# Counting edges into an adjacency matrix with other one-hots: source modulo 128 stationary, 640 keys moving

## The chip, the cores and the metric

The kernel runs on one core of one Trainium2 chip. The metric is device time in microseconds (us) for one execution, compared by the median of several runs.

## The reference, cut to what matters

Four graph layers are applied in turn, each joined to its input and normalized. All of them add up rows over the same 21250 edges, sorted by destination. The third layer tells two relations apart by `edge_type_2`.

```python
out = jax.ops.segment_sum(norm[:, None] * xw[row], col, num_segments=n)      # layer 0
agg = jax.ops.segment_sum(h[src], dst, num_segments=1250)                    # layer 1
deg = jax.ops.segment_sum(jnp.ones_like(dst), dst, num_segments=1250)
msg = jnp.where((edge_type == 0)[:, None], msgs[0], msgs[1])                 # layer 2, edge_index = (src, dst)
agg = jax.ops.segment_sum(msg, row, num_segments=1250)
x   = h + jax.ops.segment_sum(h[send], rec, num_segments=1250)               # layer 3
```

The features are 512 wide, the nodes 1250 (10 tiles of 128, padded to 1280). The weights of two relations are mixed from 30 bases: `w = einsum('rb,bio->rio', att, basis)`.

## The kernel before, in words

The kernel does not gather rows. It first builds the matrix of edge counts and then does every aggregation as a dense matmul with it. Two forms are needed: `A[p, r, t, n]`, counts for relation r with node `t*128 + p` on the partitions, and `AT`, the transposed counts summed over the relations with the identity added on the diagonal.

The counting stage works through windows of destinations. An edge list of 170 chunks of 128 edges lies in SBUF, one edge of each chunk on each partition. `window_range` (L381) reads a table that VectorE has computed: the first chunk of a window, how many pairs of chunks it spans, and a running number of pairs. For each pair VectorE writes one-hots into one of `OH` = 4 slots (`windows`, L1041): `oh_dst`, 128 wide, one-hot of destination within the window of 64 and relation; `oh_src`, 1280 wide, one-hot of the source. TensorE multiplies them (`pair_product`, L506): `oh_dst` is stationary, `oh_src` moves, and the product adds up in PSUM, 128 rows of (relation, destination) by 1280 sources, in two sets of three banks. A semaphore `s_ohu` gives slots back to VectorE, `s_oh` gives them to TensorE. ScalarE copies the finished window into `A` (`window_out`, L702) and takes the degrees `dg` as a by-product. After two windows a tile of 128 destinations is complete; TensorE turns it block by block by a matmul with the identity (`turn_counts`, L527) and ScalarE copies the result into `AT` (`turned_out`, L709).

Between the windows TensorE mixes the first layer's bases: 120 float32 products (`mix`, L543), 15 of them ahead of the first window, five after each window and the rest behind the last. They read bases that SyncE's queue brings into eight slots. VectorE also has reductions over x and W0 between windows (L1145 to L1163), ScalarE splits x into two halves, and GpSimd forms the low halves (L484, L467). Behind the stage come the unit 0 dense tiles (`dense`, L589), of which the first waits for the last mixing product's eviction, a table load and the turned input. Each engine executes its instructions in the order written; a loop over windows or pairs is a real loop with register arithmetic and a branch, and the addresses of slots and chunks are computed in registers.

Of the kernel before, what the change touches and what calls it, by code (L numbers as in the profile page):

```python
# [6 lines left out]
N, D, E = 1250, 512, 21250  # L7
# [6 lines left out]
WIN = 64  # L14
# [12 lines left out]
MIX_WIN = 5  # L27
# [16 lines left out]
def resnorm_gnn_kernel(nc, x, src_t, dst_t, typ_t, dst_r, W0, b0, gamma, beta,  # L44
# [11 lines left out]
    with ctx:  # L56
# [27 lines left out]
        dg = sb("dg", [P, REL, NT], f32)  # L84
# [28 lines left out]
        epsc = sb("epsc", [P, 1], f32)  # L113
        b0T = sb("b0T", [P, KT], f32)
# [20 lines left out]
        oh_src = zview(2 * NP * 2 * OH)  # L135
        oh_dst = zview(2 * P * 2 * OH)
        iota_n = hview(2 * NP)
        code = hview(2 * P)
        negw = hview(4 * NWIN).bitcast(f32)
        src_i, dst_i, typ_i = (wview(4 * CHUNKS).bitcast(i32) for _ in range(3))  # L140
        src_f, key_f = (wview(4 * CHUNKS).bitcast(f32) for _ in range(2))
        HC = CHUNKS // 2
        dstr = hview(4 * 2 * P).bitcast(i32).rearrange("p (g e) -> p g e", g=2)
        wlo = wview(4 * NWIN).bitcast(f32)
        whi = wview(4 * NWIN).bitcast(f32)
        cid = wview(4 * 4).bitcast(f32)
        mnx = wview(4 * 4).bitcast(f32)
        fl = wview(4 * 2 * NWIN).bitcast(f32)
# [7 lines left out]
        zview(4 * NWIN)  # L156
        mix_in = [zview(4 * D).bitcast(f32) for _ in range(MIX_SLOTS)]
# [52 lines left out]
        s_gin = sem("s_gin")  # L210
        s_xc = sem("s_xc")
# [58 lines left out]
        def tile_moved(eng, s, t, j):  # L270

            if not isinstance(t, int) or t >= 0:
                eng.wait_ge(s[j], (t + (2 - j)) * 8)

# [100 lines left out]
        Z_SCALED = 37  # L375
# [62 lines left out]
        def _(pool):  # L438
# [6 lines left out]
            pool.iota(negw, [[-2 * WIN, NWIN]], base=0, channel_multiplier=0, **kw).then_inc(s_const, 1)  # L445
            pool.iota(code, [[1, REL], [2, WIN]], base=0, channel_multiplier=0, **kw).then_inc(s_const, 1)
            pool.iota(iota_n, [[1, NP]], base=0, channel_multiplier=0, **kw).then_inc(s_const, 1)
# [6 lines left out]
            pool.memset(epsc[:, :], EPS).then_inc(s_const, 1)  # L454
            pool.memset(ones, 1.0).then_inc(b_one, 1)
# [48 lines left out]
        def _(pe):  # L504

            def pair_product(ready, slot, j, start, stop):  # L506

                pe.wait_ge(s_oh, ready)
                for q in range(2):
                    for c in range(0, NP, D):  # L510
                        w = min(D, NP - c)
                        last = nc.tensor.matmul(Df[:, j, c:c + w], oh_dst[:, ds(slot * (2 * P) + q * P, P)],  # L512
                                                oh_src[:, ds(slot * (2 * NP) + (q * NP + c), w)],
                                                start=start and q == 0, stop=stop and q == 1)
                last.then_inc(s_win if stop else s_ohu, 1)

            def window(w, j):
                _, pairs, base = window_range(pe, w)
                wait(pe, s_wev, w * 2 - 2)
# [7 lines left out]
            def turn_counts(t, g, bank=T[:, 0, :]):  # L527

                pe.wait_ge(s_wev, t * 4 + 4)
                wait(pe, s_ate, t * 3 + g)  # L530
                for q, m in enumerate(range(4 * g, min(4 * g + 4, NT))):
                    if m == t:
                        nc.tensor.matmul(bank[:, q * P:(q + 1) * P], ident[:, :], ident[:, :], start=True, stop=False)
                    for r in range(REL):
                        last = nc.tensor.matmul(bank[:, q * P:(q + 1) * P],  # L535
                                                A[:, r, ds(t, 1), m * P:(m + 1) * P].rearrange("p a c -> p (a c)"),
                                                ident[:, :], start=(r == 0 and m != t), stop=(r == REL - 1))
                last.then_inc(s_at, 1)

# [16 lines left out]
            pe.wait_ge(s_const, 9)  # L556
            pe.wait_ge(s_tbl, 1)
            for t in range(NT):
                window(2 * t, 0)
                if t:  # L560
                    turn_counts(t - 1, 0)
                mix(MIX_WIN - 2)
                if t:
                    turn_counts(t - 1, 1)
# [855 lines left out]
```

## Time and profile before

| | us |
|---|---|
| median of 3 runs (1015.02 to 1017.96) | 1015.09 |
| the profiled execution | 1016.28 |
| its span | 1014.5 |
| TensorE busy | 967.5 |
| VectorE busy | 669.1 |
| ScalarE busy | 365.7 |

The span runs from the first to the last instruction of the profiled execution; the execution's own time lies 1.8 us above it. "Busy" counts the instructions of an engine that do work, not its register, branch and semaphore instructions.

### The profile page before, as it was taken

What the parts mean: (1) busy time and instruction counts of PE and PEld (TensorE: products, weight loads), DVE (VectorE), ACT (ScalarE), POOL (GpSimd) and SP (SyncE); (2) the same over time, 40 slices, a digit from 0 to 9 for tenths busy, and PEclk for the clock granted to TensorE, in tenths of its full rate; (3) what the DMA queues carried; (4) which work ended last, traced back from release to release, by engine and by line L of the source; (5) the groups of instructions that cost most, each with busy time, mean ns of one, the idle gap of its engine ahead of it and who ended that gap; (6) DMA issues with size and microseconds to landing.
All of it is one profiled execution on the core that took longest, in us unless ns stands there. A gap on an engine that the chain in (4) does not pass through costs nothing.

```text
span 1014.5 us, 15078 instructions
## 1 busy us (share of the span) xinstructions
PE 967.5 (95%) x4904; PEld 472.2 (47%) x4904; DVE 669.1 (66%) x1262; ACT 365.7 (36%) x520; POOL 85.2 (8%) x66
## 2 busy tenths in 40 slices
PE   6899999998999799998999899999999999999997
PEld 2444444444555554444444344444444444445443
DVE  5776767664243767999999999999233334542258
ACT  0224344545587442344313322111632231144342
POOL 1000011111011100210211100000400010010000
PEclk9999999999999899999999999999999999999999
DMA  8634443444211115565553155551001003110014
GB/s 276 231 116 132 131 123 114 145 135 126 95 42 43 52 55 195 163 217 191 169 174 102 64 158 146 175 145 53 1 21 42 1 22 114 63 42 1 1 52 154
DMA packets 59445, 108.59 MB, mean 107 GB/s; under 512 B 6497, under 2 KB 6966, under 8 KB 59386
## 3 DMA queue, kind: packets, MB, share of 16 engines
q1 hardware_dynamic: 38522, 68.45, 22.0%
q10 hardware_dynamic: 20864, 39.33, 11.9%
q8 instruction: 40, 0.66, 0.3%
q14 instruction: 19, 0.16, 0.0%
HBM read 95.24 MB, written 12.52 MB: 106 GB/s over the span
## 4 chain that ended last, share of the span: by engine, by line
PE 78%; DVE 14%; DMA 3%; issue 2%; ACT 2%; POOL 1%; DVEq 0%; ACTq 0%; SPq 0%
PE Dp L610 25%; PE Dp L637 23%; PE T L551 11%; PE Dp L512 10%; PE Dp L662 4%; DVE acc L1128 4%; PE T L584 2%; PE T L535 1%; DVE stt L1219 1%; PE Dp L672 1%; DVE Zraw L1238 1%; DVE w L1256 1%; DMA Zraw<-in_basis 1%; DVE mcol L1082 1%; DVE acc L1283 1%
## 5 line engine op out<-in xcount | busy, mean ns | idle before, releaser
L610 PE MATMUL Dp<-W,hT 128*128 128x512 f16 x1320 | 296.9, 381 | 5.9 <-ACT hT L821 4.6
L610 PEld LDWEIGHTS Dp<-W,hT 128*128 128x128 f16 x1320 | 127.0, 98 | 150.9 <-ACT hT L821 6.6
L637 PE MATMUL Dp<-Zraw,A 128*128 128x512 f16 x800 | 173.3, 379 | 0.0
L1128 DVE SCALAR_TENSOR_TENSOR acc<-stage,att,acc 128x512 f32<-128x512 f32 x232 | 168.1, 792 | 1.4 <-DMA stage<-in_basis 1.4
L637 PE MATMUL Dp<-Zraw,AT 128*128 128x512 f16 x600 | 130.8, 379 | 0.5 <-DVE Zraw L1196 0.5
L551 PE MATMUL T<-Zraw,W 128*128 128x512 f32 x240 | 114.6, 615 | 10.8 <-DVE W L1011 8.5
L637 PEld LDWEIGHTS Dp<-Zraw,A 128*128 128x128 f16 x800 | 78.2, 98 | 93.9
L512 PE MATMUL Dp<-Zraw 128*128 x594 | 111.6, 343 | 3.9 <-issue 3.3
L1056 DVE TENSOR_SCALAR Zraw<-hT,w 128x1280 f16 x198 | 102.7, 561 | 0.0
L821 ACT ACTIVATE hT<-T 128x1024 f16<-128x1024 f32 x70 | 71.5, 1021 | 85.0 <-PE T L584 80.1
L1050 DVE SCALAR_TENSOR_TENSOR Zraw<-w,hT 128x256 f16 x99 | 49.8, 503 | 65.4 <-PE Dp L512 46.6
L637 PEld LDWEIGHTS Dp<-Zraw,AT 128*128 128x128 f16 x600 | 58.5, 98 | 71.0 <-DVE Zraw L1196 0.9
L512 PEld LDWEIGHTS Dp<-Zraw 128*128 x594 | 58.0, 98 | 63.0 <-issue 18.1
L1196 DVE SCALAR_TENSOR_TENSOR Zraw<-Dp,zsc,Zraw 128x512 f16<-128x512 f32 x30 | 22.5, 749 | 77.2 <-ACT Zraw L875 77.2
L1256 DVE SCALAR_TENSOR_TENSOR w<-Dp,aggc,S 128x512 f32<-128x512 f32 x40 | 29.8, 745 | 64.6 <-PE Dp L637 58.7
L705 ACT ACTIVATE A<-Dp 64x1280 f16<-64x1280 f32 x40 | 49.2, 1229 | 57.8 <-PE Dp L512 57.3
L551 PEld LDWEIGHTS T<-Zraw,W 128*128 128x128 f32 x240 | 43.5, 195 | 55.3 <-issue 44.8
L875 ACT ACTIVATE Zraw<-Dp,zsc 128x512 f16<-128x512 f32 x50 | 32.2, 686 | 92.3 <-PE Dp L610 92.0
L610 PE MATMUL Dp<-Zraw,hT 128*128 128x512 f16 x240 | 57.1, 394 | 7.1 <-ACT hT L821 6.2
L915 ACT ACTIVATE w<-w,s_in 128x512 f32<-128x512 f32 x30 | 21.6, 722 | 116.1 <-DVE w L1256 116.1
L467 POOL TENSOR_TENSOR W<-wst,W 128x1024 f16<-128x1024 f32 x18 | 42.2, 2364 | 168.2 <-ACT W L771 168.2
L584 PE MATMUL T<-ident,S 128*128 128x128 f16 x560 | 43.1, 220 | 3.9 <-ACT hT L821 3.2
(158 smaller groups left out, 772.2 us busy)
## 6 DMA issues: line engine op xcount, KB each, us to landing
Zraw<-in_basis SPq DMA_DIRECT2D x120, 256.0 KB, 3.0
stage<-in_basis SPq DMA_DIRECT2D x120, 256.0 KB, 2.9
xres<-w ACTq DMA_DIRECT2D x30, 256.0 KB, 2.0
xr<-xres ACTq DMA_DIRECT2D x30, 256.0 KB, 2.6
wst<-in_Wn ACTq DMA_DIRECT2D x4, 1024.0 KB, 5.6
wst<-in_Ws ACTq DMA_DIRECT2D x4, 1024.0 KB, 5.5
wst<-mixd ACTq DMA_DIRECT2D x4, 1024.0 KB, 5.4
wst<-in_root ACTq DMA_DIRECT2D x3, 1024.0 KB, 6.1
```

Of the source, the lines that this page charges most:

```text
L467: pool.tensor_tensor(weights_of(u, m)[:, 1, 2 * h:2 * h + 2, :], source, weights_of(u, m)[:, 0, 2 * h:2 * h + 2, :], ALU.subtract).then_in ...
L512: last = nc.tensor.matmul(Df[:, j, c:c + w], oh_dst[:, ds(slot * (2 * P) + q * P, P)], oh_src[:, ds(slot * (2 * NP) + (q * NP + c), w)], s ...
L551: nc.tensor.matmul(T[:, 1, :], mixT[:, b * P:(b + 1) * P], mix_in[n % MIX_SLOTS], start=(b == 0), stop=(b == PAIRS - 1)).then_inc(s_mx, 1)
L584: last = nc.tensor.matmul(T[:, h, k * P:(k + 1) * P], S16[:, ds(t, 1), h * D + k * P:h * D + (k + 1) * P] .rearrange("p a c -> p (a c)"), ...
L610: last = nc.tensor.matmul(Dp[:, j, m, :], hT[:, j, hp, k * P:(k + 1) * P], weights_of(u, m)[:, wp, k, :], start=(n == 0), stop=(n == 3 * K ...
L637: last = nc.tensor.matmul(sum_bank(t), a[:, k, ds(t * P, P)], Z[:, r, h, k, :], start=(n == 0), stop=(n == count - 1))
L662: last = nc.tensor.matmul(Df[:, j, c:c + w], Z[:, 0, h, k, b * P:(b + 1) * P], AT[:, k, c:c + w], start=(k == 0 and h == 0), stop=(k == NT ...
L705: nc.scalar.activation(A[WIN * j:WIN * (j + 1), r, ds(t, 1), :], Dp[WIN * r:WIN * (r + 1), j, :, :].rearrange("p j d -> p (j d)")[:, 0:NP] ...
L821: nc.scalar.activation(hT[:, j, :, :], T[:, :, :], ACT.Copy).then_inc(s_hT, 1)
L1050: v.scalar_tensor_tensor(oh_dst[:, ds(slot * (2 * P), 2 * P)].rearrange("p (c o) -> p c o", c=2), key_f[:, ds(c, 2)].rearrange("p (c o) -> ...
L1056: last = v.tensor_scalar(oh_src[:, ds(slot * (2 * NP) + q * NP, NP)], iota_n, src_f[:, ds(c + q, 1)], None, ALU.is_equal)
L1128: last = v.scalar_tensor_tensor(part, stage[:, q, :], a, part, ALU.mult, ALU.add)
```

## The change

The one-hots are cut in another way. The stationary one-hot `oh_lo` is 128 wide and marks the source modulo 128. The moving one-hot `oh_key` is 640 wide and marks a key, `20*destination + 2*(source tile) + relation`, within a window of now 32 destinations. A product has 128 rows (source within its tile) and 640 columns in two banks of 320. There are 40 windows instead of 20. A window is therefore already transposed: ScalarE copies it into a buffer `B` (two tiles deep), from which TensorE turns each relation into `A` (five steps of four blocks for a tile), and VectorE adds the two relations of `B` into `AT` and then the identity (`sum_counts`). The degrees come from ten matmuls of `AT` with a column of ones (`degrees`). The mixing products are spread evenly over the windows (`mix_share`), two or three after each.

```diff
-WIN = 64
+WIN = 32
+PER = P // WIN
+KEYS = WIN * REL * NT
+HALF = KEYS // 2
+COUNT_STEPS = ((0,), (1, 2), (3,), (4,))
...
+        def mix_share(w):
+
+            rest = PAIRS * (GROUPS - 1)
+            return (w + 1) * rest // NWIN - w * rest // NWIN
...
 # pair_product, TensorE
                 for q in range(2):
-                    for c in range(0, NP, D):
-                        w = min(D, NP - c)
-                        last = nc.tensor.matmul(Df[:, j, c:c + w], oh_dst[:, ds(slot * (2 * P) + q * P, P)],
-                                                oh_src[:, ds(slot * (2 * NP) + (q * NP + c), w)],
+                    for b in range(2):
+                        last = nc.tensor.matmul(Dp[:, j, b, 0:HALF], oh_lo[:, ds(slot * (2 * P) + q * P, P)],
+                                                oh_key[:, ds(slot * (2 * KEYS) + (q * KEYS + b * HALF), HALF)],
                                                 start=start and q == 0, stop=stop and q == 1)
...
+            def turn_counts(t, g, bank):
+
+                pe.wait_ge(s_wev, PER * (t + 1))
+                for r in range(REL):
+                    for i in range(2):
+                        last = nc.tensor.matmul(bank[:, (2 * r + i) * P:(2 * r + i + 1) * P], B[:, t % 2, 2 * g + i, r, :],
+                                                ident[:, :], start=True, stop=True)
                 last.then_inc(s_at, 1)
+
+            def degrees(t):
+
+                pe.wait_ge(s_sum, 2 * t + 2)
+                for m in range(NT):
+                    last = nc.tensor.matmul(DG[:, 2 * t:2 * t + 2], AT[:, m, t * P:(t + 1) * P], onec[:, :],
+                                            start=(m == 0), stop=(m == NT - 1))
+                last.then_inc(s_deg, 1)
...
+            for w in range(NWIN):
+                window(w, w % 2)
+                t = w // PER - 1
+                if t >= 0:
+                    for g in COUNT_STEPS[w % PER]:
+                        wait(pe, s_ate, 5 * t + g - 1)
+                        turn_counts(t, g, count_bank(t, g))
+                    if w % PER == 2:
+                        degrees(t)
+                mix(mix_share(w))
...
+            def window_out(w):
+
+                t, a = w // PER, (w % PER) * WIN
                 act.wait_ge(s_win, w + 1)
...
+                nc.scalar.activation(B[:, t % 2, :, :, a:a + WIN].rearrange("p s r (b d) -> p b (s r) d", b=2),
+                                     Dp[:, w % 2, 0:2, 0:HALF].rearrange("p b (d k) -> p b k d", k=REL * NT),
+                                     ACT.Copy).then_inc(s_wev, 1)
...
 # windows, VectorE
-                        v.scalar_tensor_tensor(oh_dst[:, ds(slot * (2 * P), 2 * P)].rearrange("p (c o) -> p c o", c=2),
-                                               key_f[:, ds(c, 2)].rearrange("p (c o) -> p c o", o=1).broadcast_to([P, 2, P]),
-                                               negw[:, ds(w, 1)],
-                                               code.rearrange("p (c o) -> p c o", c=1).broadcast_to([P, 2, P]),
-                                               ALU.add, ALU.is_equal)
                         for q in range(2):
-                            last = v.tensor_scalar(oh_src[:, ds(slot * (2 * NP) + q * NP, NP)], iota_n,
-                                                   src_f[:, ds(c + q, 1)], None, ALU.is_equal)
+                            v.tensor_scalar(oh_lo[:, ds(slot * (2 * P) + q * P, P)], iota_n[:, 0:P],
+                                            lo_f[:, ds(c + q, 1)], None, ALU.is_equal)
+                            last = v.tensor_scalar(oh_key[:, ds(slot * (2 * KEYS) + q * KEYS, KEYS)], iota_n,
+                                                   wkey[:, ds(w, 1)], key_f[:, ds(c + q, 1)], ALU.add, ALU.is_equal)
                         last.then_inc(s_oh, 1)
+
+            def sum_counts(t):
+
+                own = AT[:, t, t * P:(t + 1) * P]
+                dve.wait_ge(s_wev, PER * (t + 1))
+                v.tensor_tensor(AT[:, :, t * P:(t + 1) * P], B[:, t % 2, :, 0, :], B[:, t % 2, :, 1, :], ALU.add).then_inc(s_sum, 1)
+                dve.wait_ge(s_sum, 2 * t + 1)
+                v.tensor_tensor(own, own, ident[:, :], ALU.add).then_inc(s_sum, 1)
```

`sum_counts(t)` is called by VectorE before the third window of the tile behind t (windows 6, 10, ..., 38), and for the last tile behind all windows. Windows 6 to 9 and 13 are written out singly, the others stand in loops over two to four windows. The last tile's turns stand behind dense tiles 0 and 2 of unit 0, `degrees(9)` behind tile 0, and the square root of the degrees in ScalarE's first dense step.

The next rows are VectorE's instruction stream for one pair inside the loop over windows, from the head of the loop over pairs to its branch. This is the kernel before; "ISA", "REGISTER_ALU" and the branch are register and control rows, and "x2" stands for two alike.

```order
L1044 ISA
L1050 REGISTER_ALU
L1050 ISA
L1050 REGISTER_ALU
L1050 ISA x2
L1050 SCALAR_TENSOR_TENSOR Zraw<-w,hT 128x256
L1056 ISA
L1056 TENSOR_SCALAR Zraw<-hT,w 128x1280
L1056 ISA
L1056 TENSOR_SCALAR Zraw<-hT,w 128x1280
L1044 ISA
```

Behind these follow one register row and one branch (14 in all). The same place in the changed kernel:

```order
L1085 ISA
L1092 REGISTER_ALU
L1092 ISA
L1092 REGISTER_ALU
L1092 ISA
L1092 TENSOR_SCALAR Zraw<-hT,w 128x128
L1094 ISA x2
L1094 TENSOR_SCALAR Zraw<-hT,w 128x640
L1092 ISA
L1092 TENSOR_SCALAR Zraw<-hT,w 128x128
L1094 ISA
L1094 TENSOR_SCALAR Zraw<-hT,w 128x640
```

Behind these stand one control row, one register row and the branch (16 in all). One operation and one address row have come in for each pair; a window that is written out singly has one address row less in either kernel (13 before, 15 now).

The other place is VectorE between two windows at the end of the reductions over x. Before, between windows 6 and 7 (a row's waits stand in brackets):

```order
L1155 TENSOR_REDUCE xcol<-xr 128x1
L1158 TENSOR_REDUCE xin<-xcol 128x1 [waits s_xc]
L1042 UNCONDITIONAL_BRANCH
L383 TENSOR_LOAD tbl
L383 ISA x2
```

And in the changed kernel, between windows 9 and 10:

```order
L1213 TENSOR_REDUCE xcol<-xr 128x1
L1216 TENSOR_REDUCE xin<-xcol 128x1 [waits s_xc]
L1102 TENSOR_TENSOR AT<-Zraw 128x10x128 [waits s_wev]
L1104 TENSOR_TENSOR AT<-AT,ident 128x128 [waits s_sum]
L1083 UNCONDITIONAL_BRANCH
L1083 ISA
L406 TENSOR_LOAD tbl
L406 ISA x2
```

The two additions of `sum_counts(1)` stand ahead of the next windows' table read and one-hots; at the seven later places (before windows 14, 18, ..., 38) they stand the same way, with no reduction in front.

## Rows read from the trace of the kernel before

**Rows 1.** The page, part 1: span, and busy time and share of TensorE.

```profile
span 1014.5 us, 15078 instructions
...
PE 967.5 (95%) x4904; PEld 472.2 (47%) x4904; DVE 669.1 (66%) x1262; ACT 365.7 (36%) x520; POOL 85.2 (8%) x66
```

**Rows 2.** Stretches: length, busy us (instructions) of each engine, clock, DMA share, GB/s.

```profile
24.00:43.50 19.50, 16.50 (x72) 7.46 (x69) 12.73 (x31) 3.25 (x5) 0.00 (x0) 1.00 0.76 262
...
160.00:241.00 81.00, 78.46 (x375) 39.14 (x373) 52.97 (x103) 40.26 (x61) 13.13 (x9) 1.00 0.41 123
```

**Rows 3.** Groups by line, 0 to 290 us: busy us, mean ns, idle before.

```profile
L551 PE MATMUL T<-Zraw,W 128*128 128x512 f32 x240 | 114.6, 615 | 10.8 <-DVE W L1011 8.5 <-PE Dp L512 0.9 <-DMA Zraw<-in_basis 0.4
L512 PE MATMUL Dp<-Zraw 128*128 x594 | 111.6, 343 | 3.9 <-issue 3.3 <-DVE Zraw L1056 0.6
L1056 DVE TENSOR_SCALAR Zraw<-hT,w 128x1280 f16 x198 | 102.7, 561 | 0.0
...
L1050 DVE SCALAR_TENSOR_TENSOR Zraw<-w,hT 128x256 f16 x99 | 49.8, 503 | 65.4 <-PE Dp L512 46.6 <-issue 12.3 <-PEq L525 1.8
```

**Rows 4.** The chain of waits, 164 to 205 us: start, us, what.

```profile
170.37 5.42 PE Dp L512 x30
175.80 0.14 issue
175.93 2.81 PE T L551 x6
...
178.97 1.77 PE T L551 x4
...
186.45 0.61 PE T L535 x8
```

**Rows 5.** VectorE in order of time, 172 to 177 us: start, us, line, operation, [idle before].

```profile
172.06 0.49 DVE L1050 SCALAR_TENSOR_TENSOR Zraw<-w,hT 128x256 f16 x1 [2.95 <-PE Dp L512]
...
174.62 0.48 DVE L1050 SCALAR_TENSOR_TENSOR Zraw<-w,hT 128x256 f16 x1 [1.14 <-PE Dp L512]
175.02 1.01 DVE L1056 TENSOR_SCALAR Zraw<-hT,w 128x1280 f16 x2
176.16 0.48 DVE L1050 SCALAR_TENSOR_TENSOR Zraw<-w,hT 128x256 f16 x1
```

**Rows 6.** VectorE in order of time, first window: first pair, third and fourth.

```profile
18.72 0.48 DVE L1050 SCALAR_TENSOR_TENSOR Zraw<-w,hT 128x256 f16 x1 [2.08 <-issue]
...
22.62 0.48 DVE L1050 SCALAR_TENSOR_TENSOR Zraw<-w,hT 128x256 f16 x1 [0.33 <-issue]
...
24.38 0.48 DVE L1050 SCALAR_TENSOR_TENSOR Zraw<-w,hT 128x256 f16 x1 [0.34 <-issue]
```

**Rows 7.** VectorE in order of time, two pairs of a singly written window.

```profile
55.15 0.48 DVE L1050 SCALAR_TENSOR_TENSOR Zraw<-w,hT 128x256 f16 x1
...
56.58 0.48 DVE L1050 SCALAR_TENSOR_TENSOR Zraw<-w,hT 128x256 f16 x1
```

**Rows 8.** VectorE in order of time around the maximum of W0.

```profile
37.67 0.48 DVE L1050 SCALAR_TENSOR_TENSOR Zraw<-w,hT 128x256 f16 x1 [1.94 <-PE Dp L512]
...
41.73 0.15 DVE L1072 TENSOR_REDUCE mw<-mcol 128x1 f32<-128x1 f32 x1
43.28 0.49 DVE L1050 SCALAR_TENSOR_TENSOR Zraw<-w,hT 128x256 f16 x1 [1.39 <-issue]
```

**Rows 9.** All engines in order of time, end of the counting stage.

```profile
230.25 2.88 DVE L1056 TENSOR_SCALAR Zraw<-hT,w 128x1280 f16 x2
...
235.32 1.00 DVE L1056 TENSOR_SCALAR Zraw<-hT,w 128x1280 f16 x2
...
241.55 6.23 PE L551 MATMUL T<-Zraw,W 128*128 128x512 f32 x14
...
252.58 4.44 PE L610 MATMUL Dp<-W,hT 128*128 128x512 f16 x12
```

**Rows 10.** Groups by line, VectorE, whole span: an addition-like operation of two inputs.

```profile
L1301 DVE TENSOR_TENSOR Zraw<-Dp,W 128x1280 f32<-128x1280 f32 x4 | 6.0, 1492 | 21.2 <-PE Dp L662 21.2
```

More of the change, by code:

```diff
@@ L113, in resnorm_gnn_kernel @@
         epsc = sb("epsc", [P, 1], f32)
+        onec = sb("onec", [P, 2], f16)
         b0T = sb("b0T", [P, KT], f32)
@@ L154, in resnorm_gnn_kernel @@
         w_c = [zview(4 * NWIN).bitcast(f32) for _ in range(2)]
-        zview(4 * NWIN)
-        mix_in = [zview(4 * D).bitcast(f32) for _ in range(MIX_SLOTS)]
+        mix_in = [zview(4 * D).bitcast(f32) for _ in range(3)]
+        zview(2 * (2 * NT * D) - (2 * KEYS * 2 * OH + 2 * P * 2 * OH + 5 * 4 * NWIN + 3 * 4 * D))
+        B = zview(2 * 2 * NT * REL * P).rearrange("p (j s r c) -> p j s r c", j=2, s=NT, r=REL)
+        mix_in += [zview(4 * D).bitcast(f32) for _ in range(MIX_SLOTS - 3)]
         W2 = W[:, 2, :, :, :].rearrange("p h k d -> p (h k d)")
@@ L374, in resnorm_gnn_kernel @@
         XS_FROM = 4
-        Z_SCALED = 37
+        Z_SCALED = 40
         def halves_split(u):
@@ L618, in dense @@
                             back(BACK[t, m])
-                    if u == 0 and t < 3:
-                        turn_counts(NT - 1, t, Dp[:, 1, 2, :])
-                    if u == 0 and t == 3:
+                    if u == 0 and t == 0:
+                        degrees(NT - 1)
+                        for g in range(3):
+                            turn_counts(NT - 1, g, LAST_BANKS[g])
+                    if u == 0 and t == 2:
+                        for g in range(3, 5):
+                            pe.wait_ge(s_ate, 5 * (NT - 1) + g - 2)
+                            turn_counts(NT - 1, g, LAST_BANKS[g - 3])
+                    if u == 0 and t == 5:
+                        pe.wait_ge(s_ate, 5 * NT)
                         spread()
@@ L893, in first_z @@
                     z_out(t, j)
-                    if u == 0 and t < 3:
-                        turned_out(NT - 1, t, Dp[:, 1, 2, :])
-                    if u == 0 and t == 4:
+                    if u == 0 and t in (0, 2):
+                        for g in range(3) if t == 0 else range(3, 5):
+                            turned_out(NT - 1, g, LAST_BANKS[g % 3])
+                    if u == 0 and t == 6:
                         act.wait_ge(b_row, 1)
@@ L1141, in weight_work @@
                         scales(*what)
-            windows(0, 2)
+            windows_to(4)
             for u in (1, 3, 5):
@@ L1148, in _ @@
             weight_work("counts", 0, 0)
-            windows(2, 3)
+            windows_to(6)
             dve.wait_ge(e_x, 48)
@@ L1158, in _ @@
             v.tensor_reduce(xin[:, :], xcol[:, :], AX.X, ALU.max).then_inc(s_xin, 1)
-            windows(7, 8)
+            windows_to(13)
             dve.wait_ge(s_xmax, 1)
```

145 lines of the change are left out of this document (71 added, 74 removed).

## The prediction

> **What bounds the kernel now.** The page says it first: TensorE is busy 95% of a span of 1014.5 us, VectorE 66% [rows 1]. That is an average, so I read the stretches next. Between 160 and 241 us, in the middle of the counting stage that the change rewrites, TensorE works 78.46 of 81 us and VectorE 52.97; ScalarE works 40.26 [rows 2]. The groups of this stage show what fills TensorE: the matmuls of the one-hot pairs (L512, six to a pair, 99 pairs) and the float32 mixing of the bases (L551) [rows 3]. In the chain of waits one window of five pairs takes 5.42 us, so 1.08 us a pair, then a change-over of 0.14 us, then mixing, whose products come as two passes of 0.443 us, so 0.885 us each; the turns cost 0.61 us for eight, 0.076 us each [rows 4]. No wait for VectorE stands in that chain. The stage is TensorE's.
>
> VectorE, however, is not fast, only hidden. I read its order of time, and this is what decides the case. Within a window its pairs start 1.54 us apart (174.62, 176.16), and the first pair of the next window starts 2.56 us after the last pair of the one before (172.06, 174.62), which makes the change of window worth 1.02 us [rows 5]. The pair at 174.62 is listed as waiting for TensorE, but TensorE began this window at 170.37 and was through with the second pair, whose slot this one takes, by 172.5 [rows 4]; the cause is VectorE's own register, table and branch rows. At the start of the stage, where nothing is held back, pairs start 1.76 us apart and the engine stands idle 0.33 us in each ("issue") [rows 6]. In windows that are written out singly the distance is 1.43 us [rows 7]. So the pitch is not the length of the arithmetic. The first operation is over for its follower after 0.40 us (174.62, 175.02), two long ones of 1280 columns take 1.01 us together [rows 5], 0.56 us for one alone [rows 3], so starts 0.45 us apart; 0.40 + 0.45 + 0.45 = 1.30 us would do. What sets the pitch is the engine's own instruction stream.
>
> **The change part by part.** *Matmuls of the pairs.* A pair streams 2 x 2 x 320 = 1280 columns instead of 2560, so 0.54 us by [rows 4]. The reference's index arrays, sorted by destination, give three pairs to every one of the 40 windows: 120 in place of 99. TensorE's pairs go from 99 x 1.08 = 107 us to 120 x 0.54 = 65 us. Turns: 20 a tile where there were 21 with the diagonal, equal. New degree products, 90 inside the stage at 0.076 us or less: +7. Twenty more change-overs at 0.14 us: +3. TensorE alone would therefore save 42 - 10 = 32 us.
>
> *VectorE's pair.* Three operations become four: 128, 640, 128, 640 columns. Their arithmetic is shorter. The stream is longer: in the loop over windows 16 rows in place of 14, with one more address row and one more operation (the order shown above, row for row). One row is priced twice: 1.54 us over 14 rows is 0.11 us, and the step from the singly written loop of 13 rows to the one of 14 is 1.54 - 1.43 = 0.11 us [rows 5, 7]. Two rows more give 1.54 + 0.22 = 1.76 us a pair. Bounds: if the pushed operation costs nothing, 1.65 us; if all windows run as the first do, 1.76 + 0.22 = 1.98 us [rows 6]. I take 1.76 us for the 99 pairs in loops over several windows, 1.65 us for the 15 in windows written out singly, 1.98 us for the first six: 174.2 + 24.8 + 11.9 = 210.9 us.
>
> The opposite reading would be that register rows run behind the arithmetic of the queue, and the idle 0.33 us and the steady 1.54 us speak against it. The Trainium skill, "Advanced Engine Details and Errata", section Sequencer and Instruction Queues, states just that reading: engine instructions can be read and queued while control instructions execute. By it the pitch would be the arithmetic alone, which is the engine-paced rival below; this trace does not agree, with 1.54 us where 1.30 would do.
>
> *VectorE's change of window.* 39 instead of 19, each 1.02 us [rows 5]: 39.8 us.
>
> *The relation sum.* New on VectorE: for each of the ten tiles an addition of 128x1280 in f16, then the diagonal block, which waits for it. What follows a waiting operation shows how expensive such a stop is: after L1072 at 41.73 the next one-hot starts at 43.28, 1.55 us later, because the loop's rows only begin then [rows 8]. A sum costs its own time D, the 0.05 us to the second addition, about 0.5 us to close the old loop and that 1.55 us, less the 1.71 us that a change of window takes anyway from the last long operation's start on (2.56 less 0.40 and 0.45): D + 0.4. D is not in the trace. Nearest above: 1.49 us, the same width in f32 from PSUM [rows 10]; nearest below: 0.5 us, one of the two 1280-wide operations [rows 5]. It is f16 with two inputs, between them; I take 1.0. Nine sums inside the stage: 9 x 1.4 = 12.6 us (8 to 17). The Trainium skill, "VectorE: DVE Perf Modes", the perf-mode tier table, gives 1224 ns for 2048 elements of two 16-bit inputs in SBUF; by an estimate from that page D would be 0.8 us and the nine sums 10.8 us. No run here shows it.
>
> *Stops that were hidden.* The largest absolute value of W0 and its reduction stand between the pairs at 37.67 and 43.28, 5.61 us where 1.43 + 1.02 = 2.45 would do: 3.2 us [rows 8]. The reduction for x and the scales are two more such stops, 2.0 and 2.5 us by the same reckoning. Together 7.7 us; now TensorE's backlog covers them, afterwards nothing does.
>
> *GpSimd.* While it forms the low half of W0, two 1280-wide operations take 2.88 us instead of 1.01 [rows 9]. All four one-hot operations will be of that kind; 2 us for the collisions.
>
> *ScalarE.* 40 evictions of 640 columns instead of 40 of 1280, 50 evictions of the turned counts instead of 30. With 40 of 81 us busy now it stays far from the bound [rows 2]. No term.
>
> *Sum.* VectorE starts at 18.72 [rows 6]; one doubling step more for 40 windows, 0.4. End of its last pair: 19.1 + 210.9 + 39.8 + 12.6 + 7.7 + 2.0, less 0.5 because the last pair needs no loop end = 291.6 us, where it now is 236.3 (235.32 + 1.00) [rows 9]. TensorE follows 0.7 us later, turns (0.3) and has three products of mixing left (2.7): 295.3 us. Today the mixing ends at 241.55 + 6.23 = 247.8 [rows 9], with 14 passes after the last window; the new code spreads them, so part of VectorE's lateness is filled. Difference +47.5 us. The way from there to the first dense tile (252.58 - 247.8 = 4.8 us, [rows 9]) keeps its parts: an eviction, two DMA issues, a table load, an eviction. The degrees now come over TensorE, VectorE and ScalarE behind the first dense tile: +1, since the second tile has another bank and covers the rest. After that nothing changes. 1016.3 (the profiled execution; 1014.5 its span) + 48.5 = 1064.8. The median of the runs shown is 1.2 us lower, so 1063.5.
>
> **The rivals.** *Engine-paced (ends faster).* If VectorE's register rows hide behind its arithmetic, two starts of 640 columns at half of 0.45 to 0.45 us and two of 128 at somewhat less make a pair of 0.9 to 1.4 us, nearer the first. It then stays ahead of TensorE, and the 32 us come home: 1016.3 - 32 - 1.2 = 983. The point where it turns: the 47.5 us above vanish when the 210.9 us of pairs become 163, 1.36 us a pair. For it: the arithmetic is really shorter. Against it: the stage's steady pitch lies 0.24 us above its arithmetic, and idle "issue" stands in the first windows [rows 5, 6].
>
> *Break-even.* A pair at 1.3 to 1.4 us gives no change. It would need four operations and 16 rows to be quicker than three and 13 at 1.43 us [rows 7].
>
> *All windows in the slow pitch.* 114 pairs x 0.22 = +25 us: 1088. For it: rows 6 are rows of this same loop, at a time when VectorE was likewise the late one. Against it: 1.54 us holds in all later windows.
>
> *The clock falls.* With VectorE late, TensorE idles near 29% of the stage. At 1.2 GHz every tile of ten products of mixing and twelve pairs takes nearly twice its 18.9 us (12 x 0.54, 10.5 x 0.885, 30 x 0.076, four change-overs), 37 us against VectorE's 26.6 (12 x 1.76, 4 x 1.02, one sum): +95 us or so, 1160. Against it: between 24 and 43.5 us TensorE is in that situation already (16.50 busy of 19.50) and the granted clock stays 1.00 [rows 2].
>
> **How the numbers follow.** Forecast, VectorE bound by its instruction stream at 1.65 to 1.9 us a pair: 0.68, own range 1048 to 1078. Slow pitch throughout: 0.16. Cheaper rows, 1.45 to 1.65 us, 1022 to 1048: 0.06. Clock: 0.02. Engine-paced or near it: 0.06. Unchanged: 0.02. The range leaves out the clock, the faster case and half of the cheap one: 1040 to 1092. A difference under 0.3%, 3 us, cannot be told from none here. Slower 0.92, same 0.02, faster 0.06.
>
> **What would show it.** In the profile after, the pairs' first operation should start 1.65 to 1.9 us apart with idle "issue" between the operations; from one window's last pair to the next 2.7 to 2.9; the counting stage should end near 295 us, TensorE idle for about 30% of it, released by VectorE; pairs' matmuls at 0.54 us. The chain of waits should name VectorE in the stage where it named TensorE. Wrong would be: a pitch near 1.0 to 1.3 us, TensorE still in the chain, or a stage end below 248.

## The result, and the profile after

The kernel got slower, by about what was forecast. Its median is 1062.57 us (4 runs, 1061.3 to 1062.73) against 1015.15 us for the kernel before on the same chip (4 runs, 1015.02 to 1017.96): a ratio of 1.0456, interval 1.0441 to 1.0471. The prediction said 1063.5 us in a range of 1040 to 1092, with 0.92 for slower. The profiled execution took 1062.55 us.

I read the page of the changed kernel first: span, busy time of each engine, and the shares of the chain that ended last.

```profile
span 1060.7 us, 15792 instructions
...
PE 966.7 (91%) x4880; PEld 471.0 (44%) x4880; DVE 692.2 (65%) x1470; ACT 351.8 (33%) x501; POOL 84.5 (8%) x66
...
PE 63%; DVE 16%; issue 7%; DVEq 7%; DMA 3%; ACT 3%; POOL 0%; ACTq 0%; SPq 0%; PEldq 0%
```

TensorE's busy time looks unchanged (966.7 us, it was 967.5 [rows 1]), although the pairs stream half the columns. That is misleading, and the stretches show why (length, busy us and instructions of TensorE, its weight loads, VectorE, ScalarE and GpSimd, then clock, DMA share, GB/s; the changed kernel):

```profile
124.00:132.00 8.00, 7.73 (x32) 3.84 (x32) 4.88 (x16) 1.30 (x2) 0.00 (x0) 0.59 0.27 78
160.00:240.00 80.00, 65.30 (x306) 32.17 (x304) 52.59 (x156) 25.41 (x41) 7.61 (x7) 0.89 0.39 116
```

In the middle of the counting stage the granted clock is 0.89 where it was 1.00 [rows 2], and for some stretches it is at the lower of its two levels: 0.50 from 123.7 to 130.5 us, which gives the 0.59 of the eight microseconds from 124. Ten such stretches between 31.5 and 263.6 us add up to 58 us. So part of the "busy" time is the same work done slowly. Even with that, TensorE is busy 65.30 us of 80 there, where it was 78.46 of 81.

The groups by line of the changed kernel, 0 to 300 us (busy us, mean ns, then idle before it and what ended it):

```profile
L577 PE MATMUL T<-Zraw,W 128*128 128x512 f32 x240 | 134.1, 698 | 17.4 <-DVE W L1048 8.5 <-DMA Zraw<-in_basis 5.6 <-ACT gw L753 2.7
L534 PE MATMUL Dp<-Zraw 128*128 x480 | 84.5, 315 | 37.3 <-DVE Zraw L1094 33.4 <-issue 3.6
L1092 DVE TENSOR_SCALAR Zraw<-hT,w 128x128 f16 x240 | 65.5, 273 | 92.3 <-issue 66.6 <-PE Dp L534 16.3 <-PEq L547 9.4
```

Three figures carry the reading. The pairs' matmuls (L534) now wait 33.4 us for VectorE's one-hots; before, the pairs' matmuls waited 0.6 us for them [rows 3]. VectorE's low one-hots (L1092) have 92.3 us of idle time ahead of them, of which 66.6 us are "issue": no wait that the profile shows held the engine back; the chain below shows its own register and branch rows there. Mixing, whose code is the same, went from 114.6 [rows 3] to 134.1 us of busy time for the same 240 matmuls; that is the clock: 40 of the 240 fall in stretches at the lower level, where the median of one is 1.06 us instead of 0.59.

Next I put VectorE's instructions of the changed kernel in order of time (start, duration, line, operation, [idle before it and what ended it]). The stretch holds a change of window, a pair, a second pair, a relation sum and what follows it:

```profile
186.33 0.26 DVE L1092 TENSOR_SCALAR Zraw<-hT,w 128x128 f16 x1 [0.47 <-issue]
...
189.06 0.26 DVE L1092 TENSOR_SCALAR Zraw<-hT,w 128x128 f16 x1 [1.49 <-PE Dp L534]
189.34 0.45 DVE L1094 TENSOR_SCALAR Zraw<-hT,w 128x640 f16 x1
189.70 0.25 DVE L1092 TENSOR_SCALAR Zraw<-hT,w 128x128 f16 x1
189.86 0.44 DVE L1094 TENSOR_SCALAR Zraw<-hT,w 128x640 f16 x1
190.78 0.25 DVE L1092 TENSOR_SCALAR Zraw<-hT,w 128x128 f16 x1 [0.48 <-issue]
...
192.50 0.26 DVE L1092 TENSOR_SCALAR Zraw<-hT,w 128x128 f16 x1 [0.47 <-issue]
...
193.65 0.82 DVE L1102 TENSOR_TENSOR AT<-Zraw 128x1280 f16<-128x1280 f16 x1
194.50 0.23 DVE L1104 TENSOR_TENSOR AT<-AT,ident 128x128 f16<-128x128 f16 x1
196.13 0.26 DVE L1092 TENSOR_SCALAR Zraw<-hT,w 128x128 f16 x1 [1.41 <-issue]
```

Each pair has two L1092 rows; the first of them marks the pair's start, and the distance from one pair's start to the next is called the pitch here. Pairs start 1.72 us apart (189.06, 190.78, 192.50), the change of window takes 2.73 us (186.33 to 189.06), and one with a sum in it 3.63 us (192.50 to 196.13). The four operations need only 0.28 + 0.36 + 0.16 + 0.36 us from start to start, the last taken as the second; the rest of each pair, about 0.5 us, is idle.

The profile also shows what stands in that idle time. In the chain of waits (start, us, what; "DVEq" is VectorE's sequencer, with its register, address and branch rows) the pair at 189.06 ends like this:

```profile
189.95 0.13 issue
190.09 0.18 DVEq L1085
...
190.57 0.16 DVEq L1092
```

Between the two long rows stand three short ones of L1092 (0.04, 0.08 and 0.04 us from 190.32, 190.39 and 190.50). The last address row ends at 190.73, and the next pair's one-hot starts at 190.78.

The chain of waits says the same by engine: issue 7% and VectorE's sequencer (DVEq) 7% stand in it now. In the chain of the kernel before, TensorE had 78% and issue 2%, and its counting stage went from one TensorE product to the next [rows 4]. Between 174.7 and 189.1 us the new chain still runs over TensorE, on the strength of the name behind the wait at 189.06; further down stands why that name misleads.

The end of the counting stage, all engines in order of time, in the changed kernel:

```profile
287.37 0.44 DVE L1094 TENSOR_SCALAR Zraw<-hT,w 128x640 f16 x1
288.27 0.73 PE L534 MATMUL Dp<-Zraw 128*128 x4 [1.06 <-DVE Zraw L1094]
...
289.52 2.79 PE L577 MATMUL T<-Zraw,W 128*128 128x512 f32 x6
...
297.11 3.40 PE L633 MATMUL Dp<-W,hT 128*128 128x512 f16 x9
```

VectorE's last pair ends at 287.81 us, the mixing at 289.52 + 2.79 = 292.31, and the first dense tile starts at 297.11. Before, these were 236.3, 247.8 and 252.58 us [rows 9]. So 44.5 of the 46.2 us that the span grew have arisen by the first dense tile, and VectorE was the late engine.

### The profile page after: what moved, and what is told of

The parts are those of the page before. It is cut to its first block, busy times and chain, and to the rows that moved or that the text cites. A ratio compares the mean times of both kernels' runs of the same rounds, so it can differ in the third digit from the quotient of the medians.

```text
span 1060.7 us, 15792 instructions
## 1 busy us (share of the span) xinstructions
PE 966.7 (91%) x4880; PEld 471.0 (44%) x4880; DVE 692.2 (65%) x1470; ACT 351.8 (33%) x501; POOL 84.5 (8%) x66
## 4 chain that ended last, share of the span: by engine, by line
PE 63%; DVE 16%; issue 7%; DVEq 7%; DMA 3%; ACT 3%; POOL 0%; ACTq 0%; SPq 0%; PEldq 0%
PE Dp L633 26%; PE Dp L667 22%; PE T L577 5%; PE Dp L692 4%; DVE acc L1186 3%; DVEq L1092 3%; PE T L607 2%; DVE Zraw L1094 2%; PE Dp L534 2%; DVEq L1085 2%; DVE Zraw L1092 2%; DVEq L1094 1%; DVEq L406 1%; DVE stt L1278 1%; DVE mcol L1140 1%
## 5 line engine op out<-in xcount | busy, mean ns | idle before, releaser
L577 PE MATMUL T<-Zraw,W 128*128 128x512 f32 x240 | 134.1, 698 | 17.4 <-DVE W L1048 8.5
L1092 DVE TENSOR_SCALAR Zraw<-hT,w 128x128 f16 x240 | 65.5, 273 | 92.3 <-issue 66.6
L534 PE MATMUL Dp<-Zraw 128*128 x480 | 84.5, 315 | 37.3 <-DVE Zraw L1094 33.4
L1094 DVE TENSOR_SCALAR Zraw<-hT,w 128x640 f16 x240 | 112.5, 469 | 3.6 <-issue 0.8
L534 PEld LDWEIGHTS Dp<-Zraw 128*128 x480 | 48.3, 101 | 93.3 <-issue 74.8
L740 ACT ACTIVATE Zraw<-Dp 128x640 f16<-128x640 f32 x40 | 28.2, 704 | 180.4 <-PE Dp L534 180.4
L577 PEld LDWEIGHTS T<-Zraw,W 128*128 128x128 f32 x240 | 48.8, 220 | 67.3 <-issue 50.8
L950 ACT ACTIVATE w<-w,s_in 128x512 f32<-128x512 f32 x30 | 21.6, 721 | 116.4 <-DVE w L1315 116.4
```

Source lines behind the costliest of these rows:

```text
L534: last = nc.tensor.matmul(Dp[:, j, b, 0:HALF], oh_lo[:, ds(slot * (2 * P) + q * P, P)], oh_key[:, ds(slot * (2 * KEYS) + (q * KEYS + b * H ...
L577: nc.tensor.matmul(T[:, 1, :], mixT[:, b * P:(b + 1) * P], mix_in[n % MIX_SLOTS], start=(b == 0), stop=(b == PAIRS - 1)).then_inc(s_mx, 1)
L1092: v.tensor_scalar(oh_lo[:, ds(slot * (2 * P) + q * P, P)], iota_n[:, 0:P], lo_f[:, ds(c + q, 1)], None, ALU.is_equal)
L1094: last = v.tensor_scalar(oh_key[:, ds(slot * (2 * KEYS) + q * KEYS, KEYS)], iota_n, wkey[:, ds(w, 1)], key_f[:, ds(c + q, 1)], ALU.add, AL ...
```

## The experiments

All ratios are against the kernel before on the same chip. Theory A is the prediction's: the pairs' pitch is set by VectorE's own instruction stream. Its rivals are arithmetic (the operations' lengths) and waiting for TensorE or for a buffer.

**Arithmetic taken away.** Each key one-hot writes 64 columns instead of 640; the slots are set to zero once at the start. Rows of the stream, waits, matmuls and everything behind them stay. The counts leave out most edges.

```diff
-  last = v.tensor_scalar(oh_key[:, ds(slot * (2 * KEYS) + q * KEYS, KEYS)], iota_n,
+  last = v.tensor_scalar(oh_key[:, ds(slot * (2 * KEYS) + q * KEYS, 64)], iota_n[:, 0:64],
```

> The changed kernel with every key one-hot cut from 640 to 64 columns; the other 576 columns of each slot stay zero, so most edges are not counted. The rows of VectorE's stream stay the same, its arithmetic shrinks. If the instruction stream sets the pitch, pairs stay 1.72 us apart and the time is within 3 us of 1062.6. If the arithmetic sets it, each 640-wide operation falls from 0.36 us to about 0.16 between starts, a pair from 1.72 to 1.3 us, and 120 pairs give back 45 us or more: 1015.

Measured: 1059.28 us (1056.86 to 1060.56), before 1016.38, ratio 1.0419 (1.0397 to 1.044). VectorE in order of time, one pair and the next's start:

```profile
189.56 0.25 DVE L1093 TENSOR_SCALAR Zraw<-hT,w 128x128 f16 x1 [0.77 <-issue]
189.83 0.30 DVE L1095 TENSOR_SCALAR Zraw<-hT,w 128x64 f16 x1
...
191.26 0.25 DVE L1093 TENSOR_SCALAR Zraw<-hT,w 128x128 f16 x1 [0.77 <-issue]
```

The key one-hot's own row fell from 0.45 to 0.30 us, and the idle time grew from 0.48 to 0.77 us: the pairs still start 1.70 to 1.74 us apart. Operations that need nothing like 1.7 us do not start sooner. The stage starts 0.6 us later, because the slots are cleared first, and still the first dense tile comes 2.4 us earlier (294.68 against 297.11). Two single places account for 2.5 of these 3.0 us: a wait for a free slot at 36 us that is shorter by 1.5 us, and the collision with GpSimd at 269 us, shorter by 1.0 us. Arithmetic is ruled out as what sets the pitch.

**Rows taken away.** The two low one-hots of a pair are formed by one operation of 256 columns, as the kernel before forms its source one-hots. Two rows of the stream less in each pair; the result is the same.

```diff
+  v.scalar_tensor_tensor(oh_lo[2 chunks], lo_f[:, ds(c, 2)] broadcast, 0.0,
+                         iota_n[:, 0:P] broadcast, ALU.add, ALU.is_equal)
   for q in range(2):
-      v.tensor_scalar(oh_lo[one chunk], iota_n[:, 0:P], lo_f[:, ds(c + q, 1)], None, ALU.is_equal)
       last = v.tensor_scalar(oh_key[one chunk], iota_n, ...)
```

> The changed kernel with both 128-wide one-hots of a pair written by one operation of 256 columns: 14 rows of the stream for a pair instead of 16, three operations instead of four, but about 0.1 us more arithmetic (0.40 us to its follower instead of two times 0.16). Stream theory: pitch 1.72 - 0.2 = 1.5 us, 120 pairs, 1062.6 - 22 = 1040. Arithmetic theory: 1062.6 + 10 = 1073.

Measured: 1038.77 us (1037.13 to 1040.89), before 1016.38, ratio 1.0216 (1.0199 to 1.0233), 23.8 us less than the changed kernel. VectorE in order of time:

```profile
187.80 0.42 DVE L1091 SCALAR_TENSOR_TENSOR Zraw<-w,hT 128x256 f16 x1 [0.56 <-issue]
188.15 0.80 DVE L1097 TENSOR_SCALAR Zraw<-hT,w 128x640 f16 x2
189.34 0.43 DVE L1091 SCALAR_TENSOR_TENSOR Zraw<-w,hT 128x256 f16 x1 [0.39 <-issue]
...
190.85 0.42 DVE L1091 SCALAR_TENSOR_TENSOR Zraw<-w,hT 128x256 f16 x1 [0.38 <-issue]
```

Pairs start 1.51 to 1.54 us apart. That is the kernel before's pitch of 1.54 us [rows 5] with the same number of rows, though its long operations had 1280 columns and these have 640.

**Rows added.** One more operation of two columns at the head of each pair, into a spare buffer, with its address row; the result is the same.

```diff
+  v.tensor_scalar(spare[:, ds(slot * 2, 2)], iota_n[:, 0:2], lo_f[:, ds(c, 1)], None, ALU.is_equal)
   for q in range(2):
```

> The changed kernel with one more operation a pair, two columns wide, into two spare columns: two more rows of the stream (18), 0.06 to 0.16 us of arithmetic, less than the 0.48 us that the engine idles in each pair. Stream theory: +0.2 us a pair, 1062.6 + 24 = 1087. Arithmetic theory: hidden in the idle time, 1062 to 1064.

Measured: 1080.16 us (1079.22 to 1081.68), before 1016.38, ratio 1.0633 (1.0616 to 1.0651), 17.6 us more. VectorE in order of time, two pair starts:

```profile
189.65 0.23 DVE L1092 TENSOR_SCALAR Zraw<-hT,w 128x2 f16 x1 [0.49 <-issue]
...
191.52 0.23 DVE L1092 TENSOR_SCALAR Zraw<-hT,w 128x2 f16 x1 [0.48 <-issue]
```

The pitch is 1.87 us, and the idle time has stayed at 0.48: two rows cost 0.15 us here. The forecast of 24 us was too high, since it took 0.2 us a pair. Four windows of this run (14 to 17, counted from 0) are slower still, 2.10 us a pair; the last section comes back to them.

**The relation sum's second addition.** In the loop, the diagonal block's addition waits for the sum. Here it is taken out of the loop, and the identity is added once by two strided operations behind the stage (the degrees get their one by a separate addition); the result is the same.

```diff
   (in sum_counts, ten times)
-  dve.wait_ge(s_sum, 2 * t + 1)
-  v.tensor_tensor(own, own, ident[:, :], ALU.add).then_inc(s_sum, 1)
   (behind the stage, once)
+  v.tensor_tensor(blocks, blocks, one, ALU.add).then_inc(s_sum, 1)
+  v.tensor_tensor(tail, tail, ident[:, :], ALU.add).then_inc(s_sum, 1)
```

> The changed kernel with the identity added to all ten diagonal blocks behind the stage by two operations, so that no addition inside the stage waits for the sum in front of it; the degrees get their one in a separate addition. If such a wait holds back the whole stream, the nine changes of window with a sum fall from 3.65 us to the plain 2.73, so 9 x 0.9 = 8 us less, about 1 us comes back behind the stage: 1055. If the sum's own 0.82 us is what costs, only the second addition's 0.2 us goes: 1061.

Measured: 1054.93 us (1054.2 to 1055.8), before 1016.38, ratio 1.0383 (1.0366 to 1.04), 7.6 us less than the changed kernel. VectorE in order of time:

```profile
188.48 0.25 DVE L1092 TENSOR_SCALAR Zraw<-hT,w 128x128 f16 x1 [0.47 <-issue]
...
189.63 0.82 DVE L1101 TENSOR_TENSOR AT<-Zraw 128x1280 f16<-128x1280 f16 x1
191.21 0.25 DVE L1092 TENSOR_SCALAR Zraw<-hT,w 128x128 f16 x1 [0.77 <-PEq L547]
```

From the last pair to the next window it takes 2.73 us with the 0.82 us sum in it, exactly what a change of window takes without one. The sum's arithmetic runs while the stream's rows go on and costs nothing. What cost 0.9 us was the wait behind it: it holds the stream until the sum is done, and only then do the rows for the next window start. These distances are the evidence, more than the total: nine times 0.92 are 8.3 us, while the first dense tile comes 9.8 us earlier (287.36), because a collision with GpSimd is some 2.8 us shorter and one loop of four windows some 1.7 us longer than in the changed kernel.

**Cover put over it.** The extra operation of the third experiment, put into the kernel before, where TensorE is the bound. Its pairs then have 17 rows in the loops over windows, three more than before and one more than the changed kernel's 16: two of address and register work, and the operation.

```diff
+  v.tensor_scalar(spare[:, ds(slot * 2, 2)], iota_n[:, 0:2], src_f[:, ds(c, 1)], None, ALU.is_equal)
```

> The kernel before with one more operation a pair, two columns wide, three more rows in VectorE's stream (17 for 14). VectorE then needs 5 x 1.85 + 1.02 = 10.3 us a window against TensorE's 10.8. If VectorE's stream is hidden behind TensorE here, the time stays within 3 us of 1015.2. If the stage already hung on VectorE's pace, 99 x 0.3 = 30 us come on top: 1045.

Measured: 1018.47 us (10 runs, 1016.83 to 1019.07), before 1015.23 (13 runs), ratio 1.0026 (1.0017 to 1.0036). VectorE in order of time:

```profile
189.28 0.48 DVE L1050 SCALAR_TENSOR_TENSOR Zraw<-w,hT 128x256 f16 x1 [0.21 <-issue]
189.68 0.22 DVE L1055 TENSOR_SCALAR Zraw<-hT,w 128x2 f16 x1
...
191.03 0.48 DVE L1050 SCALAR_TENSOR_TENSOR Zraw<-w,hT 128x256 f16 x1 [0.22 <-issue]
```

The pitch rose from 1.54 to 1.75 us, a little over the changed kernel's 1.72, and the time by 3 us. Unhidden, 99 pairs at 0.21 us would have been 21 us. So it is not the slower pitch alone that made the changed kernel slow, but the slower pitch together with the cover that it lost: TensorE's five pairs of 1.08 us and its mixing held up a window longer than VectorE's rows took.

**Fewer starts of the loop.** If the stream's rows are the price, they should be paid once for six chunks instead of three times for two. With these index arrays every window has exactly six. One slot per window: one operation of 768 columns for the low one-hots, six of 640 for the keys, one semaphore exchange, one group of twelve matmuls. It contains the late diagonal too; three buffers for incoming bases had to move to make room, and SyncE's loads of the later bases wait for the end of the mixing. It would need a loop for windows with more chunks.

```diff
-OH = 4
+OH = 2
+SIX = 6
-        oh_key = zview(2 * KEYS * 2 * OH)
-        oh_lo = zview(2 * P * 2 * OH)
+        oh_key = zview(2 * KEYS * SIX * OH)
+        oh_lo = zview(2 * P * SIX * OH)
-        mix_in = [zview(4 * D).bitcast(f32) for _ in range(3)]
+        mix_in = [stage[:, q, :] for q in range(3)]
...
-                        for q in range(2):
-                            v.tensor_scalar(oh_lo[one chunk], ...)
-                            last = v.tensor_scalar(oh_key[one chunk], ...)
+                        v.scalar_tensor_tensor(oh_lo[6 chunks], ...)
+                        for q in range(SIX):
+                            last = v.tensor_scalar(oh_key[one chunk], ...)
```

> The changed kernel, late identity included, with all six chunks of a window in one slot (two slots): one operation of 768 columns for the low one-hots, six of 640 for the keys, one loop body a window in place of three, and one product of twelve matmuls on TensorE. It takes six chunks for every window, which is what these index arrays need in all 40. VectorE's stream falls from 3 x 16 rows to about 22 a window; its arithmetic stays, 3.1 us a window. Stream theory: VectorE needs about 4 us a window against TensorE's 4.7, TensorE becomes the bound again and the matmul saving of 32 us comes home: 985, range 978 to 1000, clock near full in the stage. Arithmetic theory: no gain beyond the late identity, 1055.

Measured: 996.08 us (993.12 to 997.17), before 1015.23, ratio 0.981 (0.9792 to 0.9828). It beats both kernels. The stretch from 110 to 240 us, then VectorE and TensorE in order of time:

```profile
110.00:240.00 130.00, 115.64 (x658) 61.44 (x657) 87.53 (x180) 59.78 (x93) 17.64 (x12) 0.99 0.45 140
```

```profile
171.84 1.94 PE L576 MATMUL T<-Zraw,W 128*128 128x512 f32 x4
...
181.24 0.96 DVE L1091 SCALAR_TENSOR_TENSOR Zraw<-w,hT 128x768 f16 x1 [2.13 <-PEq L546]
...
183.78 1.79 PE L536 MATMUL Dp<-Zraw 128*128 x12
...
190.40 1.08 PE L576 MATMUL T<-Zraw,W 128*128 128x512 f32 x2
```

VectorE now waits 2.13 us for TensorE before a window, and TensorE runs product after product: one window's twelve matmuls in 1.79 us, a whole tile from 171.84 to 190.40, 18.56 us. The prediction's count was 18.9 (its terms add up to 18.6); the kernel before takes 21.6 (from one such place at 170.21 to the next at 191.80). The clock is back at 0.99. The forecast, 985 us, was missed by 11. Here is a part of it, TensorE of the same kernel in order of time:

```profile
30.68 2.04 PE L576 MATMUL T<-Zraw,W 128*128 128x512 f32 x2 [5.17 <-DMA Zraw<-in_basis]
```

TensorE comes to the next bases before they have landed, and stands still for 5.17 us. This is not new with the six chunks. In the chain of waits of the changed kernel, too, the start of the stage hangs on this transfer:

```profile
22.07 9.66 DMA Zraw<-in_basis
31.87 3.48 PE T L577 x4
```

There TensorE stood still for 5.63 us. The kernel before had one-hot products to do until 31.04 us and waited 0.36. With six chunks, ten tiles at 3.0 us saved, less 5.2, are 25 us; the first dense tile starts at 228.40 against 252.58, 24.2 us earlier. The span is 23.2 us shorter (991.3). This execution was the quickest of its kernel, 993.12 us; by the medians the gain is 19.2 us, and what differs between the executions no trace here shows. Of the 11 us missed, the wait for the bases is 5.2, the tiles' saving is 30 us where the forecast had 32, and 3.0 lie between this execution and the median; about 1 is left open.

**The same without mixing behind the first two windows.** The planner's quota of mixing products starts with the third window.

```diff
+        def mixed_by(w):
+            return max(0, w - 2) * PAIRS * (GROUPS - 1) // (NWIN - 2)
```

> The kernel with six chunks a slot, and no mixing product behind the first two windows; the 105 products are spread over the other 38. In the run before, TensorE stood idle from 25.5 to 30.7 us for the next bases, which queue behind the load of x. If that idle time is what keeps the stage 5 us short of TensorE's own saving, the time falls by 3 to 5 us, to 991 to 993. If the bases' transfers are late in the whole stage, or VectorE is late at its start, nothing changes: 996.

Measured: 992.33 us (990.7 to 993.65), before 1016.91 (8 runs), ratio 0.9757 (0.974 to 0.9774), against 0.981 (0.9792 to 0.9828) for the one before; the intervals do not meet. TensorE in order of time:

```profile
26.40 1.89 PE L538 MATMUL Dp<-Zraw 128*128 x12 [1.50 <-DVE Zraw L1099]
29.73 1.89 PE L538 MATMUL Dp<-Zraw 128*128 x12 [1.44 <-DVE Zraw L1099]
```

The wait for the bases is gone; two waits for VectorE of 1.50 and 1.44 us stand where mixing had been. The first dense tile starts at 225.70, 2.7 us earlier (5.17 less 2.94 are 2.2).

## Why the prediction was right

By the terms of its sum, in microseconds:

| term | predicted | measured in the changed kernel |
|---|---|---|
| first one-hot starts | 19.1 | 19.06 |
| pairs in loops over windows, 99 | 1.76 each | 1.72 each |
| pairs in windows written out singly, 15 | 1.65 each | 1.65 each |
| pairs in the first two windows, 6 | 1.98 each | 1.92 each |
| all 120 pairs | 210.9 | 206.6 |
| change of window, 39 | 1.02 each, 39.8 | 1.01 each, 39.4 |
| relation sums, 9 | 1.4 each, 12.6 | 0.92 each, 8.3 |
| stops that had been hidden | 7.7 | about 7.4 |
| collisions with GpSimd | 2.0 | 3.6 at one place, more in all |
| last pair ends | 291.6 | 287.81 |
| mixing ends | 295.3 | 292.3 |
| against the kernel before | +47.5 | +44.5 |

*The pitch.* Right, and for the reason given. Arithmetic cut to a fraction left 1.72 us; two rows less gave 1.51 to 1.54; two more gave 1.87. The slope over these three is 0.08 to 0.10 us a row, under the 0.11 that the prediction had worked out, which is why 1.76 became 1.72. A row has no single price, though: the extra operation in the kernel before brought three rows for 0.21 us, and in the chain above single rows take 0.04 to 0.18 us.

The prediction set aside the reading by which operations run while register rows are handled, since 1.54 us stood where 1.30 would do. That was too strong. The two do run side by side: the row of L1085 shown above stands from 190.09 to 190.27 us, while the one-hot that started at 189.86 runs until 190.30. The pitch is the longer of the two streams, and in both kernels that is the rows. The last section shows the other case.

*The change of window.* Right to 0.01 us, and so is what was said of it: the one-hot at 189.06 shows 1.49 us of idle time with a name of TensorE's behind it, but by the trace its last address row ended only at 189.00, and the distances are the same where TensorE is at half its clock and where it is not. Of the 16.3 us that L1092 is put down as waiting for the pairs' matmuls only one place is a real wait: the second pair of the third window starts 3.48 us after the first instead of 1.72, at 36.40, because TensorE had come late out of the mixing, where it had waited 5.63 us for the bases. The prediction has no term for this wait; it cost VectorE 1.8 us.

*The relation sum.* The mechanism was right, the size too large, and this is the term most off for its size: 0.92 us instead of 1.4. Its duration D, which no row of before had, is 0.82 us, where I took 1.0 between bounds of 0.5 and 1.49. The estimate of 0.8 from the Trainium skill, "VectorE: DVE Perf Modes", the perf-mode tier table, was nearer: this trace agrees with it. The other 0.3 us come mostly from what was subtracted: from the start of a window's last operation to the next window a plain change takes 1.93 us (2.73 less 0.80), not 1.71. The loop also closed in 0.36 us instead of 0.5. The rest was nearly right: 0.85 us from the sum's start to the second addition and 1.63 us on to the next one-hot (193.65, 194.50, 196.13). Taking the second addition away removed exactly this 0.92 us.

*The hidden stops.* Right. Around the maximum of W0 the distance is 5.53 us (it was 5.61 [rows 8]) where a change of window takes 2.73: 2.8. The two reductions for x, counted beyond a sum and a change, come to 1.2 and 1.4 us, the scales to 2.0.

*GpSimd.* Too small. Where it forms the low half of W0, the distance from one window to the next with a sum in it is 7.21 us instead of 3.65. VectorE in order of time:

```profile
269.43 1.68 DVE L1092 TENSOR_SCALAR Zraw<-hT,w 128x128 f16 x1 [0.41 <-issue]
271.02 2.29 DVE L1094 TENSOR_SCALAR Zraw<-hT,w 128x640 f16 x1
```

Two operations of 0.26 and 0.45 us take 1.68 and 2.29. Smaller stretchings elsewhere, a slow window (8) and the real wait at 36.40 add some 4 us. The too small and the too large terms largely cancel, which is luck and no merit.

*The first windows.* Taken from a row, 1.98 us, and right to 0.06 from the second distance on (the very first is 2.32). Why they are slower is still open (below).

*TensorE.* Ten degree products take 0.25 us (in the chain, 178.41), 0.025 us each and not 0.076, which saves 5 of the 7 us put down for them and changes nothing while TensorE is not the bound. Its pairs are as predicted, 0.54 to 0.55 us in a row of three (12 matmuls in 1.65 us in the chain, at the full clock). The predicted idle of about 30% of the stage is 18% by the records, 14.7 of 80 us, and here the step "the clock stays 1.00" was wrong. That rival got 0.02, and its condition came in part: the clock fell, in stretches, while VectorE was late. What it said of the time did not follow. It had counted every tile at the lower level, 37 us, and only stretches were, 58 of the 232 us from 31.5 to 263.6. VectorE's distances over the stretch from 124 us, where mixing passes take 0.9 us instead of 0.44, are 1.73, 1.71 and 2.74 us, the same as elsewhere. The idle time that the pitch left TensorE paid for the lower clock.

*The other rivals.* Engine-paced and break-even fell with the narrow one-hots. The slow pitch throughout did not come: the first two windows run at 1.92, and one of those written out singly (8) has distances of 2.21 and 1.86 where the others have 1.65.

*Behind the stage.* Predicted +1 us for the degrees; the aggregation starts 45.4 us later, so 0.9 more than the 44.5 of the first dense tile. The span grew by another 0.8 us after that, which I did not look for.

The experiments took and added rows only together with their operation. That an address row by itself costs time is shown by the windows written out singly, whose pairs have the same operations and one address row less: 1.43 against 1.54 us in the kernel before, 1.65 against 1.72 in the changed kernel, 1.80 against 1.88 with the extra operation. So one such row costs 0.07 to 0.11 us.

## What to carry to other kernels

An engine in the shadow of another has a price that its busy share does not show: measure the distance from start to start in its loop, not the operations' lengths, and ask whether that distance still fits if the covering engine gets faster. A change that halves columns but adds an operation makes such a loop slower; the remedy was to pay the loop's rows once for more work, 1.9% and, with the mixing moved, 2.4% under the kernel before. Inside such a loop a wait costs more than the operation behind it.

## What the runs showed of the hardware

**Operations and rows run side by side, and the longer stream sets the pitch.** Held up by GpSimd, VectorE catches up. The changed kernel, in order of time:

```profile
198.14 1.27 DVE L1094 TENSOR_SCALAR Zraw<-hT,w 128x640 f16 x1
199.33 0.24 DVE L1092 TENSOR_SCALAR Zraw<-hT,w 128x128 f16 x1
...
199.85 0.24 DVE L1092 TENSOR_SCALAR Zraw<-hT,w 128x128 f16 x1
```

The operation at 198.14 took 1.27 us beside a GpSimd operation at 198.07, and the one-hots behind it, already issued, then start every 0.52 us, 1.04 us for a pair. So the arithmetic's own pace is 1.04 us where the steady pitch is 1.72. The delay is won back whole: that window's three distances are 1.74, 1.98 and 2.47, against 1.73, 1.71 and 2.73 undisturbed. In this kernel only the collision at 269 us, beside 4.2 us of GpSimd's work, is felt.

**Some loops are slower, each as a whole.** In the first two windows of the stage the pitch is 1.92 us instead of 1.72. VectorE in order of time:

```profile
21.38 0.26 DVE L1092 TENSOR_SCALAR Zraw<-hT,w 128x128 f16 x1 [0.64 <-issue]
21.78 0.45 DVE L1094 TENSOR_SCALAR Zraw<-hT,w 128x640 f16 x1
...
23.30 0.26 DVE L1092 TENSOR_SCALAR Zraw<-hT,w 128x128 f16 x1 [0.55 <-issue]
```

Even inside the pair the second operation follows after 0.40 us instead of 0.28. The same +0.22 us stands in the kernel before (1.76 against 1.54) and in it with the extra operation (1.98 against 1.76). But the start of the stage is not what the slow windows have in common. In the changed kernel with the extra operation, windows 14 to 17 have it:

```profile
132.77 0.23 DVE L1092 TENSOR_SCALAR Zraw<-hT,w 128x2 f16 x1 [0.62 <-issue]
...
134.87 0.23 DVE L1092 TENSOR_SCALAR Zraw<-hT,w 128x2 f16 x1 [0.61 <-issue]
```

The pitch is 2.10 to 2.12 us there, where 1.87 to 1.91 stand in the windows around them. With the late diagonal it is windows 18 to 21 (1.93 us instead of 1.71). Windows 0 and 1, 14 to 17 and 18 to 21 are each one loop of the program, and in these three every window of the loop is slow. No run tells why.

**The clock at a moderate load.** In the changed kernel the granted clock was 0.50 from 123.7 to 130.5 us, the lower of its two levels (1.2 GHz), and at that level for 58 of the 232 us from 31.5 to 263.6, in a stage where TensorE's idle time comes in pieces of a microsecond or so (14.7 of 80 us over some 13 windows). In the kernel with six chunks a slot it idles 14.4 of 130 us, and the clock stays at 0.99; in the kernel before, between 24 and 43.5 us, it idled 3.0 of 19.5 and had 1.00 [rows 2]. I had not expected a fall at this load.
